# Weight loads in two groups, the shared keys and weight sums inside pass -1, and another order table for the first loop of a two-layer token kernel

## The reference

```python
h = concat([tok(x), txt], axis=1)                      # 16 x 324 x 192
h = h + attn0(layernorm(h))     # softmax over tokens, circular product with the values, projection
h = h + ffn0(layernorm(h))      # 192 -> 768, gelu, 768 -> 192
h = h + attn1(layernorm(h))     # 12 heads; keys and values also of 196 shared tokens (sc_token)
h = h + ffn1(layernorm(h))      # 4 experts pick 162 of 324 tokens each; MLP and a 12-head attention inside
```

## Time and profile before

| | us |
|---|---|
| median of 3 runs | 2244.34 (2236.84 to 2247.42) |
| the profiled execution | 2232.77, span 2231.1 |
| PE busy | 1903.3 (85%) |
| DVE busy | 1416.2 (63%) |
| ACT busy | 1109.0 (50%) |
| POOL busy | 260.7 (12%) |
| first loop's first patch matmul | starts at 72.70 |
| first yT of the second loop | starts at 1534.39 |

### The profile page before, as it was taken

The page is one execution under the profiler, slowest core; times in us unless marked ns, Lnnn a source line. Parts: engine busy times, 40 slices in busy tenths (PEclk is TensorE's granted clock), DMA queues, the critical chain, the costliest instruction groups (busy, mean ns, idle before and its releaser), DMA issues. The chain is left out here.

```text
span 2231.1 us, 45808 instructions
## 1 busy us (share of the span) xinstructions
PE 1903.3 (85%) x11896; PEld 1275.0 (57%) x11896; DVE 1416.2 (63%) x4501; ACT 1109.0 (50%) x2577; POOL 260.7 (12%) x404
## 2 busy tenths in 40 slices
PE   0368899889999999989999988832999999999996
PEld 0245566566666666656656655421666666666664
DVE  2236677677678677777777766524566656656663
ACT  0024545545545545545545554410656656666663
POOL 3010010011011011011011001000010100100100
PEclk9679999999999999999999998855999999999998
DMA  4020220221221121121022021002243343333431
GB/s 135 14 53 1 59 56 25 58 54 33 49 54 42 40 62 44 35 59 54 24 60 57 20 59 50 26 24 67 64 117 90 95 103 95 101 91 99 116 81 34
DMA packets 157284, 133.82 MB, mean 60 GB/s; under 512 B 31760, under 2 KB 136480, under 8 KB 157088
## 3 DMA queue, kind: packets, MB, share of 16 engines
q1 hardware_dynamic: 153472, 127.46, 21.8%
q0 software_dynamic: 2304, 4.79, 0.8%
q10 hardware_dynamic: 1440, 0.75, 0.1%
HBM read 81.52 MB, written 50.16 MB: 59 GB/s over the span
## 5 line engine op out<-in xcount | busy, mean ns | idle before, releaser
L1018 DVE TENSOR_REDUCE mxh<-mps 108x1 f32<-108x260 f32 (+1 forms) x1728 | 683.2, 443 | 344.6 <-PE mps L1179 333.1
L780 ACT ACTIVATE prob<-sps 108x324 f32<-108x324 f32 x1536 | 624.6, 440 | 501.3 <-PE sps L1157 455.9
L1157 PE MATMUL sps<-qpack,kpack 128*108 128x324 bf16 x1536 | 445.9, 326 | 34.4 <-ACT prob L780 27.9
L1179 PE MATMUL mps<-kpack,qpack 96*108 96x260 bf16 (+1 forms) x1728 | 415.6, 297 | 45.5 <-DMA kpack<-scr_k 26.8
L1179 PEld LDWEIGHTS mps<-kpack,qpack 96*108 96x108 bf16 x1728 | 220.0, 130 | 192.2 <-DVE mxh L1018 77.2
L1170 PE MATMUL aps<-prob,v 128*32 128x324 f32 x3072 | 324.2, 466 | 3.1 <-PEq L130 2.3
L1157 PEld LDWEIGHTS sps<-qpack,kpack 128*108 128x108 bf16 x1536 | 193.3, 130 | 221.9 <-ACT prob L780 162.6
L1147 PE MATMUL lin<-yT,w 128*128 128x324 f32 x576 | 183.5, 452 | 8.3 <-DVE yT L1063 7.6
L618 POOL CAST piece<-rest 128x324 bf16<-128x324 f32 x96 | 43.7, 456 | 782.0 <-DVE rest L889 769.1
L1170 PEld LDWEIGHTS aps<-prob,v 128*32 128x32 f32 x3072 | 74.4, 110 | 105.0 <-issue 56.4
L1147 PEld LDWEIGHTS lin<-yT,w 128*128 128x128 f32 x576 | 103.6, 193 | 51.8 <-issue 11.7
(11 more groups left out here) (156 smaller groups left out, 2445.3 us busy)
## 6 DMA issues: line engine op xcount, KB each, us to landing
qpack<-scr_q SPq DMA_DIRECT2D x96, 243.0 KB, 3.3
kpack<-scr_k SPq DMA_DIRECT2D x96, 121.5 KB, 3.4
scr_q<-piece SPq DMA_DIRECT2D x32, 243.0 KB, 2.9
scr_k<-piece SPq DMA_DIRECT2D x32, 243.0 KB, 3.6
kpack<-scr_k SPq DMA_DIRECT2D x96, 81.0 KB, 3.2
bc<-rec_d SPq DMA_DIRECT2D x128, 60.8 KB, 2.3
scr_q<-piece SPq DMA_DIRECT2D x32, 162.0 KB, 3.2
scr_q<-piece SPq DMA_DIRECT2D x64, 81.0 KB, 3.1
```

Of the source, the lines that this page charges most:

```text
L780: nc.scalar.activation(prob[0:rows, n % NP, :], sps[0:rows, n % 2, 0:N], ACT.Exp, scale=SCALE).then_inc(att.exped.sem, 1)
L1018: nc.vector.tensor_reduce(mxh[:, hd, t, s:s + 1], att.mps.at(use)[0:P, 0:att.width], AX.X, ALU.max, negate=True).then_inc(att.mps.free["dv ...
L1157: mm(sps[0:rows, n % 2, 0:N], kpack[:, 4 * q + n % 4, k * att.rows:k * att.rows + rows], qpack[:, 4 * q + n % 4, :], start=True, stop=True ...
L1179: mm(bank[0:P, 0:att.width], qpack[0:6 * D, 4 * q + hd, t * P:(t + 1) * P], kpack[0:6 * D, 4 * q + hd, s * att.width:(s + 1) * att.width], ...
```

## The change

- **Loads.** FIRST holds the eight things that passes -2 and -1 use up to attn0's projection, on a semaphore of its own (loads_first). The rest follows on loads. w_p1 and w_2a's halves are laid out with their gaps by the host, so that one load each takes the place of 36. The second halves of the weights land in prob instead of g and av.
- **Order of the start.** POOL issues the load of image 0 first, then 10 memsets. PE, before pass -2, waits for loads_first, six memsets of DVE and one of POOL; PE and ACT wait for all loads between pass -2 and pass -1.
- **Shared keys.** A new word, shared, stands in slot 0 and runs in pass -1 alone: PE's 16 matmuls (into mps and sps instead of lin and mps), ACT's and DVE's and POOL's pieces, SP's way through DRAM. PE waits for their end ahead of the first m (shared_in).
- **Sums of weights.** On POOL behind its pieces (both_layers) instead of DVE, with prob's memset; the first s waits for them.
- **begin.** In the first pass of each loop all items ahead of the first step that has an image are left out on every engine; the semaphores' first values are raised by as much (passed).
- **The table.** ORDER_1 is another one: same words, same offsets, other order. ORDER_2 is unchanged.

The diff, cut:

```diff
 ORDER_1 = (
-    "a ln2_1 m m m s v_0.0 s ln2_2 ln2_3 s s m v_0.1 m s m v_1.0 s recip s",
-    "t2_0 m a m s t2_1 m m s",
-    "m s a s m hid0 m hid1 pack2",
-    "m hid2 hid3 s m s m hid4 m m norm a m",
-    "hid5 m m s s m proj4_0.0 m den m proj4_0.1 s spread0 spread1 proj4_1 s s ln4_0 a s hx ln4_1 r ln4_2 s",
-    "out_0.0 m m out_0.1 a m out_0.2 m ln4_3 out_0.3 m out_1.0 m out_1.1",
-    "s m s ln3_0 tok.0 s tok.1 m m m s hab t4_0 t4_1 ln3_1 s m hb m a m log m s t5_0",
-    "exp m ln3_2 s s ln3_3 t5_1 s m m s a",
-    "s prob m t3_0 hc m s t3_1 m a ln1_0 m qk0 m m qk1 s m s qk2 s s ln1_1 r",
-    "s todram s prt a s s",
-    "a s t1_0 t1_1 s s ln1_2 ln1_3 zv s",
-    "val_0.0 zs val_0.1 s val_1 pack0 zt s m m m dft_0.0 m m xload pack1 m a m s m m dft_0.1 m s m m dft_1.0 m m",
-    "m dft_1.1 s m of s a s",
-    "s m s m m a s inv_0.0 s m m s m s m m s",
-    "inv_0.1 inv_1.0 inv_1.1 s r proj_0.0 proj_0.1 proj_1 s ln2_0 a",
+    "s ln2_1 v_0.0 ln2_2 shared s s a s s m v_0.1 ln2_3 m m s",
+    "v_1.0 m s s t2_0 a recip t2_1 m s den",
+    "m m pack2 a s m s hid0 m m hid1 m",
+    "m hid2 m m m hid3 m s m m s m norm hid4 hid5 m m a m s m m proj4_0.0 proj4_0.1 spread0 s s proj4_1 spread1 hx",
+    "out_0.0 ln4_0 a s r out_0.1 s out_0.2 ln4_1 s ln4_2 s ln4_3",
+    "m m out_0.3 a m s s out_1.0 m m out_1.1 m tok.0 ln3_0",
+    "m s m tok.1 m s m a t4_0 ln3_1 m t4_1 hb t5_0 m s s m m t5_1 m ln3_2 ln3_3",
+    "s log m s s m a s t3_0 hab t3_1",
+    "ln1_0 exp hc m prob s s m todram m qk0 m qk1 m s m qk2 s s m ln1_1 ln1_2 pack0 s a s",
+    "s r s ln1_3 s prt a",
+    "a t1_0 t1_1 pack1 s s zv zs val_0.0 val_0.1 val_1 s m m zt m m s",
+    "m dft_0.0 m m m s dft_0.1 m m a m s m s",
+    "m dft_1.0 m s m m dft_1.1 m s m m s s a s s of",
+    "m a xload s m s s m s inv_0.0 m s",
+    "m inv_0.1 inv_1.0 inv_1.1 r a s proj_0.0 proj_0.1 proj_1 ln2_0 s",
 )
...
+                offset = offsets.get(step, offsets.get(base(step)))
+                if self.begin is None and offset is not None and has(first + offset, 0, B - 1):
+                    self.begin, lin_passed, mps_passed = len(self.items), len(lin_uses), len(mps_uses)
...
+        self.lin.passed(lin_passed)
+        self.mps.passed(mps_passed)
...
-            for kind, what, part in att.items:
+            for n, (kind, what, part) in enumerate(att.items):
+                if isinstance(i, int) and i == att.first_pass and n < att.begin:
+                    continue
...
+                elif what == "shared":
+                    if isinstance(i, int) and i == -1:
+                        step(what, 0, 0, what, None, i)
...
+        def loops(eng, run, second, between=None):
 
             for i in range(-1 if second else -2, 1):
                 run(i)
+                if i == -2 and between:
+                    between()
...
 
-        SETUP_POOL, SETUP_DVE = 12, 11
+        MEMSETS_POOL, SETUP_POOL, SETUP_DVE = 10, 14, 7
         block = ctx.enter_context(nc.Block())
 
+        FIRST = [(w_tok, A["w_tok"]), (ident, A["ident"]), (w_a, A["w_a"]), (w_v0, A["w_v0"]), (dft, A["dft"]),
+                 (idft, A["idft"]), (w_p0, A["w_p0"])]
         LOADS = [
-            (w_tok, A["w_tok"]), (w_a, A["w_a"]), (w_v0, A["w_v0"]), (w_p0, A["w_p0"]),
-            (w_in, A["w_in"]), (b_in, A["b_in"]), (w_out, A["w_out"]), (w_qkv, A["w_qkv"]),
-            (w_r, A["w_r"]), (gamma, A["gamma"]), (beta, A["beta"]), (w_1, A["w_1"]),
-            (ident, A["ident"]), (dft, A["dft"]), (idft, A["idft"]),
+            (w_in, A["w_in"]), (b_in, A["b_in"]), (w_qkv, A["w_qkv"]), (w_out, A["w_out"]),
+            (w_r, A["w_r"]), (gamma, A["gamma"]), (beta, A["beta"]), (w_p1, A["w_p1"]), (w_1, A["w_1"]),
             (cum, A["cum"]), (cum8, A["cum8"])]
-        NLOAD = len(LOADS) + 2 + 3 * H + 3 + 1
+        NFIRST, NLOAD = len(FIRST) + 1, len(LOADS) + 7
+        w_2s = prob[:, 0:6, 0:C]
+        w_2as = prob[:, 6:9, 0:C]
 
         def tiles2(bank):
...
             for s in primed:
-                sp.sem_inc(s.sem, s.at(s.first, 0))
-            for dst, src in LOADS:
+                sp.sem_inc(s.sem, s.at(s.first, 0) + s.passed)
+            for dst, src in FIRST:
+                sp.dma_start(dst.ap(), src).then_inc(loads_first.sem, 16)
+            sp.dma_start(b_p0[:, :], A["b_p0"].partition_broadcast(P)).then_inc(loads_first.sem, 16)
+            for dst, src in LOADS[:4]:
+                sp.dma_start(dst.ap(), src).then_inc(loads.sem, 16)
+            sp.dma_start(xS[0:KC, :, N:NK1], A["sc"]).then_inc(loads.sem, 16)
+            for dst, src in LOADS[4:]:
                 sp.dma_start(dst.ap(), src).then_inc(loads.sem, 16)
             sp.dma_start(w_2[:, :, :], A["w_2"][:, 0]).then_inc(loads.sem, 16)
-            sp.dma_start(g[:, :, 0:C], A["w_2"][:, 1]).then_inc(loads.sem, 16)
-
-            sp.wait_ge(setup_pool.sem, 2)
-            for hd in range(H):
-                r = 32 * (hd % 4)
-                sp.dma_start(w_p1[r:r + D, hd // 4, :], A["w_p1"][hd * D:(hd + 1) * D, :]).then_inc(loads.sem, 16)
-                for s, dst in enumerate((w_2a, av[:, :, 0:C])):
-                    sp.dma_start(dst[r:r + D, hd // 4, :],
-                                 A["w_2a"][s, hd * D:(hd + 1) * D, :]).then_inc(loads.sem, 16)
-            sp.dma_start(b_p0[:, :], A["b_p0"].partition_broadcast(P)).then_inc(loads.sem, 16)
+            sp.dma_start(w_2s, A["w_2"][:, 1]).then_inc(loads.sem, 16)
+            sp.dma_start(w_2a[:, :, :], A["w_2a"][0]).then_inc(loads.sem, 16)
+            sp.dma_start(w_2as, A["w_2a"][1]).then_inc(loads.sem, 16)
             sp.dma_start(b_p1[:, :], A["b_p1"].partition_broadcast(P)).then_inc(loads.sem, 16)
             sp.dma_start(b_2[:, :, :], A["b_2"].partition_broadcast(P)).then_inc(loads.sem, 16)
-            sp.dma_start(xS[0:KC, :, N:NK1], A["sc"]).then_inc(loads.sem, 16)
-            sp.wait_ge(setup_dve.sem, SETUP_DVE)
-            sp.wait_ge(setup_pool.sem, SETUP_POOL)
-
-            sp.wait_ge(sc_pieces.sem, 2)
-            for m in range(2):
-                sp.dma_start(scr_k[:, 128 * m:128 * m + SCK[m], 0:SC].rearrange("s p n -> p s n"),
-                             piece[0:SCK[m], m, :, 0:SC]).then_inc(sc_scr.sem, 16)
-            sp.wait_ge(sc_scr.sem, 32)
-            for r, s in enumerate(K_PARTS):
-                sp.dma_start(kpack[r * D:(r + 1) * D, :, N:NK1],
-                             scr_k[s, :, 0:SC].rearrange("(d h) n -> d h n", d=D)).then_inc(sc_pack.sem, 16)
-            sp.wait_ge(sc_pack.sem, 16 * 6)
+
+            def shared_keys():
+
+                sp.wait_ge(setup_pool.sem, MEMSETS_POOL)
+                sp.wait_ge(sc_pieces.sem, 2)
+                for m in range(2):
+                    sp.dma_start(scr_k[:, 128 * m:128 * m + SCK[m], 0:SC].rearrange("s p n -> p s n"),
+                                 piece[0:SCK[m], m, :, 0:SC]).then_inc(sc_scr.sem, 16)
+                sp.wait_ge(sc_scr.sem, 32)
+                for r, s in enumerate(K_PARTS):
+                    sp.dma_start(kpack[r * D:(r + 1) * D, :, N:NK1],
+                                 scr_k[s, :, 0:SC].rearrange("(d h) n -> d h n", d=D)).then_inc(sc_pack.sem, 16)
+                sp.wait_ge(sc_pack.sem, 16 * 6)
 
             def to_dram(att, j):
...
         def _(pool):
-            for n, (x, value) in enumerate(((w_p1[:, :, :], 0.0), (w_2a[:, :, :], 0.0), (xS[KC:KP, :, :], 0.0),
-                                            (v1[:, :, :, :], 0.0), (kpack[KC:KP, :, :], 0.0),
-                                            (yA[KC:KP, :, :], 0.0), (v1[:, 0:KT1 - 1, :, D:D + 1], 1.0),
-                                            (v1[0:LAST1, KT1 - 1, :, D:D + 1], 1.0),
-                                            (kpack[6 * D:6 * D + 3, :, :], 1.0),
-                                            (yA[KC:KC + 1, :, :], 1.0), (of[64:KP, :, :, :], 0.0), (bc[:, :, :], 1.0))):
-                if n:
-                    pool.wait_ge(setup_pool.sem, n)
-                nc.gpsimd.memset(x, value).then_inc(setup_pool.sem, 1)
-            for m, p in enumerate(SCK):
-                pool.wait_ge(sc_rest.sem, m + 1)
-                nc.gpsimd.tensor_copy(piece[0:p, m, 1, 0:SC], rest[0:p, m, 0:SC]).then_inc(sc_mid.sem, 1)
-                pool.wait_ge(sc_mid.sem, m + 1)
-                nc.gpsimd.tensor_tensor(piece[0:p, m, 2, 0:SC], rest[0:p, m, 0:SC], piece[0:p, m, 1, 0:SC],
-                                        ALU.subtract).then_inc(sc_pieces.sem, 1)
-            pool.wait_ge(loads.sem, 16 * NLOAD)
...
-
             def load_x(j):
                 pool.dma_start(pT[:, :, :], A["x"][j]).then_inc(x_in.sem, 16)
                 pool.dma_start(hin[IMG - P:P, 1, :], A["txt"][j, 0:2 * P - IMG, :]).then_inc(x_in.sem, 16)
                 pool.dma_start(hin[:, 2, :], A["txt"][j, 2 * P - IMG:TXT, :]).then_inc(x_in.sem, 16)
 
             load_x(0)
+            for n, (x, value) in enumerate(((of[64:KP, :, :, :], 0.0), (xS[KC:KP, :, :], 0.0), (v1[:, :, :, :], 0.0),
```

(28 more changed lines are left out.)

144 lines of the change are left out of this document (88 added, 56 removed).

## The result

Median 2186.21 us over four runs (2184.14 to 2190.63) against 2243.9 for the kernel before on the same chip: ratio 0.9749, 95% interval 0.972 to 0.9779, so 57.7 us faster. The forecast was 2177 (67 us faster), with 2150 to 2212 as its range. The profiled execution took 2184.14 (span 2182.1), 2 us under its median; that of before lay 11 us under its own.

The account below looks back on a forecast made before the run. PE's queue and the chains it waits for bound the loop; load issues, sums, shared keys and a walk bound the opening. Opening -56.4, table -12, last pass +1.5 make -67 us: 2244.3 to 2177 us, range 2150 to 2212.

Parts of the forecast that it names:

- The opening: Before the first patch matmul: start at 14.0 us (bounds 12.5 and 22) instead of 72.7, 58.7 us earlier.
- The second group: Remaining loads behind the first group: 5.73 MB at 375 GB/s end near 28 us, 20 us of slack, cost nothing.
- The table load of ACT: ACT's first table load, moved from the setup to between first patches and their layernorm: 1.28 us added on the path.
- The shared keys: Pass -1, PE between proj and t2: 16 matmuls, 5.5 us, fit into idle time; DVE's added work costs 1.0 us.
- The sums on POOL: Pass -1: 8 us with prob's memset, hidden ahead of hb, cost nothing; one blocked DVE instruction (up to 2.8 us) left out.
- The table: New order in the first loop: pass from 81.4 to 80.6 us, -0.8 us each, -12 us over 15 full passes.
- Segment 3: First dft to proj: chains as before, 0.7 us more work within; 16.1 us instead of 15.9.
- segment 2: t1 to the first dft: m waits about 1.8 us for kpack, more m behind it; 8.1 us instead of 6.8.
- Segment 6: First out to t3: ln4 keeps DVE from m, outs 9.3 instead of 7.4, later stretch 9.5 instead of 10.9; 18.8 us.
- The last pass: log behind t5 costs about 2.5 us, PE's walk before prt gets shorter by five m: +1.5 us, bounds 0 and 3.
- the second loop: Table stays and begin drops some steps of its pass -1, hidden by DVE's wait for cntb: 0.
- Rival A: Opening as forecast, table worth nothing or costing 0 to 2 us a pass through the kpack wait: 2189 to 2219; chance 0.23.

Follow-up runs that it names:

- run 4: The changed kernel, but PE waits for all loads before pass -2; 2199.15 us, first patch matmul 17.0 us later than with two groups.
- after_with_old_table: The changed kernel with ORDER_1 of the kernel before, the word shared put between ln2_2 and ln2_3; 2194.2 us, 0.9777 of before.
- runs 1 and 7: 1 is after_with_old_table; 7 moved POOL's sums behind the xload of pass -1, on the changed kernel (2174.79 us) and on after_with_old_table (2179.62 us).
- run 2: The kernel before with only the new ORDER_1, without the word shared; 2247.2 us against 2244.8, ratio 1.0011.
- run 10: The changed kernel with the m ahead of the first dft part, the first of which waits for kpack, moved behind it; 2159.83 us.
- run 9: The changed kernel with POOL's step hab two slots forward, ahead of hb instead of behind it; 2167.17 us against 2234.54 for before.
- Run 8: The changed kernel with the old table, sums later, and ln2_2 and shared ahead of the three m of slot 0; 2189.2 us, 0.9811 of before.
- run 6: The kernel before executed once more, unchanged, for the spread between executions; 2235.99 us, span 2234.3 beside 2231.1.
- run 3: The changed kernel with begin at 0, so pass -2 walks over all its steps again; 2203.35 us.

## Why the prediction was right where it was, and wrong where it was not

**The opening: right.** Forecast for the first patch matmul 14.0 us, measured 15.23, ended by the load named (b_p0, the last of the first group). That is 57.5 us gained instead of 58.7. The second group was through at 32.2 (run 4), not near 28 as worked out from its rate, and still far ahead of PE's need of it. The walk and the wait for all loads, each put back by itself, measured 12.4 us (11 forecast) and 17.0 us. proj of pass -2 came at 47.53, forecast near 48.

**The table load of ACT: wrong, small.** +1.3 us was charged; it ran at 5.09, while ACT waited for PE, and cost nothing. The step that failed is that a load stands behind the wait of the operation that needs it; here it stood ahead. The Trainium skill (ScalarE: Activation LUTs, What ACT_TABLE_LOAD costs) gives 1283 ns for it and more for a drain behind; the row has 1.28 us, and no drain could be seen.

**The shared keys: right in place, wrong in size.** They took 1.71 + 1.55 us and not 5.5: in before they ran at 0.39 and 0.30 us a matmul behind a PE that had done nothing for 45 us, here at 0.21 and 0.19 behind a busy one. In after_with_old_table, with 3.56 us of idle ahead, the first eight take 3.13 us again. tok to hc(-1) grew by 3.4 us in the profile of after and by -0.4 to 1.1 in the four others whose passes -2 and -1 hold the same steps ahead of that copy (61.8 to 63.3); forecast were 2.3.

**The sums on POOL: right for this table, by luck of the cover.** "DVE has nearly nothing to do there once ln2_3 is through" holds with the new table, where the layernorm ends at 57.6 and the sums begin at 58.10. Half a microsecond is the cover. With the old table it is gone, and one DVE operation alone takes 5.17 us beside the same sums; moving them brought hc(-1) forward by 8.1 us, most of it by this (runs 1 and 7). The prediction had the row that warned of it and named 2.8 us for one blocked instruction; what it left out is that POOL's sums stand back to back, and the one operation outlasted two of them.

**The table: the failed step.** Forecast -0.8 us a pass, measured +0.44 in the profile and nothing in the timed runs (run 2). By the prediction's segments, measured in one pass of after (first out at 884.75 to first out at 966.64; rows of PE's timeline):

| segment | before | forecast | after |
|---|---|---|---|
| 1 qk2 end to t1 | 7.2 | 6.9 | 6.85 |
| 2 t1 to dft | 6.8 | 8.1 | 7.65 |
| 3 dft to proj | 15.9 | 16.1 | 17.3 |
| 4 proj to t2 | 8.8 | 8.3 | 8.1 |
| 5 t2 to out | 18.4 | 16.9 | 16.5 |
| 6 out to t3 | 18.2 | 18.8 | 19.85 |
| 7 t3 to qk2 end | 6.0 | 5.5 | 5.7 |

Five are within 0.5 us. Two carry the miss. Segment 3 is 1.2 longer than forecast: the kpack wait of segment 2 was foreseen (1.8 us, measured 17.3 in ten passes), but not that PE's clock can be lower in the stretch behind it; two dft parts of this pass take 1.3 us more than at full clock, and in run 10 the wait and the slow parts are gone together. Segment 6 is 1.05 longer: m waits once for DVE's maximum behind the second t4:

```profile
901.03 0.32 PE L1241 MATMUL mps<-kpack,qpack 96*108 96x260 bf16 x1 [1.08 <-DVE mxh L1064]
```

The prediction had named this place (DVE with ln4, eleven m and ln3 in one queue) and made the segment 0.6 us longer for it, not 1.65. It counted POOL's hb, hab and hc, now in one block beside ln3, as part of a stretch that gets shorter, and put their effect on DVE at nothing. That was the step that failed here: with hab moved away 0.65 of the 1.08 us are gone, and 0.60 come back where hab stands then (run 9). For the 0.43 that are left no run moved a layernorm out of the stretch. Run 8 shows on the old table that a layernorm ahead of three m costs such waits, which speaks for DVE's own queue but doesn't show it here.

**The last pass: too little.** +1.5 forecast for the step from hc(14) to yT, measured +3.8. PE's walk over steps without an image did not get shorter ahead of prt; it grew from 3.82 to 4.65 us, and the one ahead of t4 from 8.33 to 9.74:

```profile
1434.52 1.28 PE L1178 MATMUL lin<-ident,xna 108*96 108x108 f32 x6 [9.74 <-PEq L136]
...
1444.43 0.70 PE L1350 MATMUL lin<-ident,pr 108*4 108x108 f32 x3 [4.65 <-PEq L136]
```

**The sum.** Against the profiled run, 2166 was forecast and 2184.1 measured. The 18 us: 1.2 at tok, 1.1 up to hc(-1), 11.2 in the fifteen passes (-0.8 measured, -12 forecast), 2.3 in the last pass, 2.1 in the second loop, which is within the spread of run 6. Against the medians only 9 us are missing, since the profiled run of before lay 11.6 us below its median and that of after 2: carrying the distance over was wrong as a method and happened to help. Rival A, with 0.23, was the one whose mechanism held: kpack's wait takes in what the other segments give back, as it said. Its time, 2189 to 2219, begins just above the measured median, which lies in the forecast's own range of 2160 to 2190: the total came out in range with the table's term wrong, because the opening is most of it. By the segments' own figures before adds up to 81.3 us, not 81.4, which changes nothing here.

## What to carry to other kernels

A wait costs its own length and sometimes a slower stretch behind it (about 1 us a pass in the dft matmuls of after, none behind some longer waits): look at the matmuls that follow a new wait, and try first to put work ahead of it that doesn't need what it waits for (run 10: 1.1 to 1.5 us a pass for two lines of the table). A total of waits can stay the same while one wait goes and another comes: go through them one by one before calling a cause dead (run 9). Waits saved in a hand-ordered pipeline come back at the next queue that was just in time, so list the arrivals with their slack before judging a new order by the waits it removes. In an opening, look for issues, walks and a wait for more than is needed; each gave 11 to 17 us here, and unlike the table they can be added up from rows.

## What the hardware showed that was not expected

- Three DVE operations of 0.32 us each took 5.80 us together beside POOL's back-to-back sums of 2.60 and 1.39 us, the last of them 5.17 alone, and 0.96 elsewhere; moving the sums brought hc(-1) forward by 8.1 us, most of it by this.
- DVE operations on 108x3 elements took 0.46 to 0.52 us beside POOL's hb and hab and 0.16 elsewhere.
- The granted clock was 0.72 in the 6 us behind a wait of 1.27 us (after, at 923.34), and 1.00 behind one of 1.90 us in another pass of the same execution (at 430.20), with the same steps ahead. So the length of the wait doesn't decide by itself.
- Steps of waits and increments without any work cost 12.4 us at the start (run 3); in the last pass PE's sequencer held it for 9.74 and 4.65 us over such steps.
- ACT's table load of 1.28 us ran at 5.09 us, 13 us before the operation that needed it.
